# A two-layer decoder in one kernel: where the causal attention's projections, the head scalings and three of the layer norms stand in the program

## The reference, cut to what matters

```
# layer 0, first block: a linear recurrence over the 1024 tokens, then a small network
h = _ln(x, ln1_g, ln1_b); spec = einsum(h, W_to); real, imag = halves of spec
def step(carry, u):
    sr = sr * decay + r * 0.1;  si = si * decay + i * 0.1
    nr = clip(sr * c - si * s, -10, 10);  ni = clip(sr * s + si * c, -10, 10)
x2 = x + 0.1 * einsum(out_r|out_i, W_from)
h = _ln(x2, ln3_g, ln3_b); h = gelu(h @ W_ffn1.T + b1) @ W_ffn2.T + b2
return x2 + 0.1 * h                       # then x = _layernorm(x + this)
# layer 0, second block: cross attention, 16 heads of 16, over 154 context rows
# layer 1, first block: causal attention, 16 heads of 64 over 1024 tokens
att = where(causal, q k^T / 64, -inf); y = softmax(att) v; z = einsum(W, y) / 8
x = _layernorm(x + z)
```

## Time and profile before

| | us |
|---|---|
| median of three runs | 2289.43 |
| the profiled execution, its own time | 2288.46 |
| its span | 2286.7 |
| recurrence stage, while VectorE steps (61.8 to 623.5) | 561.7 |
| rest of the recurrence stage (to 711) | 87.5 |
| causal stage (904 to 1665) | 761 |

### The profile page before, as it was taken

The page is one execution under the profiler, slowest core; times in us unless marked ns, Lnnn a source line. Parts: engine busy times, 40 slices in busy tenths (PEclk is TensorE's granted clock), DMA queues, the critical chain, the costliest instruction groups (busy, mean ns, idle before and its releaser), DMA issues.

```text
span 2286.7 us, 34566 instructions
## 1 busy us (share of the span) xinstructions
PE 1815.0 (79%) x12969; PEld 1302.1 (57%) x12969; DVE 1445.2 (63%) x4633; ACT 934.0 (41%) x2211; POOL 501.3 (22%) x554
## 2 busy tenths in 40 slices
PE   4447666776677868998999789989887999998808
PEld 1335555655564435665666566666665899884306
DVE  4887787778723685565555345555654666663595
ACT  3413323332334742444444224444513555553662
POOL 3011110111010012333233223333321333330002
PEclk9667777877887987999999999999999999999958
DMA  4000000000000012000000000000032333310001
...
DMA packets 86312, 49.82 MB, mean 22 GB/s; under 512 B 40205, under 2 KB 83905, under 8 KB 85953
## 3 DMA queue, kind: packets, MB, share of 16 engines
...
q10 hardware_dynamic: 6784, 0.56, 0.3%
...
## 4 chain that ended last, share of the span: by engine, by line
PE 56%; DVE 23%; ACT 10%; issue 3%; POOL 2%; POOLq 0%; DVEq 0%; ACTq 0%
PE PS L1501 6%; PE PS L1795 5%; PE PS L1531 5%; PE PS L1518 4%; DVE sq L645 4%; DVE nx L642 4%; ACT px L1569 3%; PE PS L1468 3%; PE PS L1486 3%; PE PS L1476 3%; PE PS L2208 2%; PE PS L1546 2%; PE PS L1858 2%; PE PS L852 2%; PE PS L1814 2%
## 5 line engine op out<-in xcount | busy, mean ns | idle before, releaser
L1651 POOL TENSOR_SCALAR px<-px,crl 128x128 f32<-128x128 f32 (+7 forms) x128 | 239.8, 1874 | 461.1 <-DVE crl L1627 461.1
L1569 ACT ACTIVATE px<-PS,cnm 128x128 f32<-128x128 f32 (+7 forms) x256 | 187.6, 737 | 252.0 <-DVE cnm L1611 252.0
L1611 DVE TENSOR_REDUCE cnm<-PS 128x1 f32<-128x128 f32 (+7 forms) x256 | 181.9, 752 | 82.0 <-PE PS L1506 81.9
L182 POOL TENSOR_SCALAR rstd<-mv 128x1 f32<-128x1 f32 x128 | 41.3, 323 | 866.5 <-DVE mv L161 866.4
L645 DVE TENSOR_SCALAR sq<-nx 128x4 f32<-128x4 f32 x1024 | 183.1, 179 | 35.0
L642 DVE TENSOR_TENSOR_SCAN nx<-sq 128x6 f32<-128x6 f32 x1024 | 181.8, 178 | 34.7 <-SPq L2275 2.3
L1518 PE MATMUL PS<-ident,px 128*128 128x128 f32 x1152 | 160.5, 280 | 35.3 <-DVE pT L1619 33.5
L1518 PEld LDWEIGHTS PS<-ident,px 128*128 128x128 f32 x1152 | 130.7, 143 | 81.2 <-DVE pT L1619 37.3
L1501 PE MATMUL PS<-kT,qT 64*128 64x512 f32 (+3 forms) x768 | 159.5, 519 | 14.5 <-ACT px L1569 14.5
L1531 PE MATMUL PS<-pT,V 128*64 128x128 f32 x2304 | 159.1, 285 | 5.4 <-DVE pT L1619 5.3
L1885 ACT ACTIVATE YT<-YT,xnm 128x154 f32<-128x154 f32 x256 | 104.8, 414 | 92.9 <-DVE xnm L1927 92.9
...
## 6 DMA issues: line engine op xcount, KB each, us to landing
...
```

The source lines that it names most:

```text
L1569: e.activation(k.px[n % 2][:, h, 0:width], src, ACT.Exp, bias=k.cnm[:, n % 4, h:h + 1], accum_out=k.cl[:, n % 4, h:h + 1]).then_inc(sem("c ...
L1611: e.tensor_reduce(k.cnm[:, n % 4, h:h + 1], src, AX.X, ALU.max, negate=True).then_inc(sem("c.max"), 1)
L1651: e.tensor_scalar(k.px[n % 2][:, 0, 0:width], k.px[n % 2][:, 0, 0:width], k.crl[:, n % 4, 0:1], None, ALU.mult).then_inc(sem("c.normal0"), 1)
```

## The change

Three edits, and some semaphores that are shared.

1. **Norms 1, 2 and 3 change engine.** For these, VectorE's `unit` goes. GpSimd gets `shift`, which computes minus mean times reciprocal root (one 128x1 instruction), and ScalarE gets `side`, which applies scale and shift as one activation on 128x256.
2. **The recurrence's chains.** The norm's list reads r, stats, aggr, shift, 5 steps later side, 2 steps later turn and put. The end of "sums" (r 3 and its norm) becomes a fourth chain, "ends", offered 20 steps after `out`, and `out` comes 4 steps after `back`.
3. **The causal stage.** `cn` is parted by head: head 0's reciprocal stays ahead of `ct`'s copies, and head 1's reciprocal and scaling go behind them. The projections get fixed units: in units 2, 3, 4 of a pair its own second half, in 5, 6, 7 the next pair's first half. The 8 output tiles of batch 0 are spread, with `zout` and statistics in one unit, `unit` in the next and `turn` and `put` in the one after. The weight flips `wz` go to units 0 and 1 of pairs 1 and 2, and unit 0 of pair 3.

Semaphores `ident` and `rec.zero` go; what waited for them waits for `zeroed` and `zero`, the last of which is signalled after GpSimd's other opening memsets.

```
@@ norm_vector, norm_pool, norm_scalar @@
-        dst = k.xs4[:, lane, :] if L in (0, 1, 7) else k.xt(T)
+        dst = k.xs4[:, lane, :] if L in (0, 7) else k.xt(T)
+    def shift(L, T):
+        rs = k.rstd[:, lane_of(L, T), :]
+        w.wait_ge("ln.rstd", at("aggr", L, T))
+        e.tensor_scalar(rs[:, 0:1], k.mv[:, lane_of(L, T), 0:1], rs[:, 1:2], -1.0, ALU.mult, ALU.mult).then_inc(sem("ln.shift"), 1)
+    def side(L, T):
+        lane = lane_of(L, T)
+        w.wait_ge("ln.shift", at("shift", L, T))
+        if L == 1:
+            w.wait_ge("ln.turn", k.turn_before.get((L, T), 0))
+        dst = k.xs4[:, lane, :] if L == 1 else k.xt(T)
+        e.activation(dst, k.r4[:, lane, :], ACT.Identity, scale=k.rstd[:, lane, 1:2], bias=k.rstd[:, lane, 0:1]).then_inc(sem("ln.side"), 1)
@@ recurrence_order, network_chain, near_sums @@
+        needs["r", 3, T] = [("n.out", T)]
+    ends = Chain(o, needs, [step for T in k.near_tiles for step in near_ends(T)])
...
-        for kind, wait in (("r", gap), ("stats", 0), ("aggr", 0), ("unit", 5), ("turn", 0), ("put", 0)):
+        for kind, wait in (("r", gap), ("stats", 0), ("aggr", 0), ("shift", 0), ("side", 5), ("turn", 2), ("put", 0)):
...
-    yield 0, ("n.out", T)
-    yield 11, ("r", 3, T)
+    yield 4, ("n.out", T)
+
+
+def near_ends(T):
+    yield 20, ("r", 3, T)
     yield 1, ("stats", 3, T)
     yield 1, ("aggr", 3, T)
-    yield 5, ("unit", 3, T)
+    yield 0, ("shift", 3, T)
+    yield 6, ("side", 3, T)
@@ causal_order @@
-    def prepare(u):
-        return [[("cq", u, 0)], [("ck", u, 0)], [("cv", u, 0)], [("cq", u, 1)], [("ck", u, 1)], [("cv", u, 1)]]
...
+    for u in range(2 * HP):
+        for i, kind in enumerate(("cq", "ck", "cv")):
+            beside[u, 2 + i].append((kind, u, 1))
+            if u + 1 < 2 * HP:
+                beside[u, 5 + i].append((kind, u + 1, 0))
+    for x, steps in zip(((1, 0), (1, 1), (2, 0), (2, 1), (3, 0)), wz):
+        beside[x] += steps
+    for T in range(BT):
+        chain = list(norm_chain(5, T))
+        n = HP * BT + 2 + (0, 1, 1, 2, 3, 4, 5, 6)[T]
+        beside[units[n]] += [("zout", T), *chain[:3]]
+        beside[units[n + 1]].append(chain[3])
+        beside[units[n + 2]] += chain[4:]
+    o.add(("cq", 0, 0), ("ck", 0, 0), ("cv", 0, 0))
+    for n, x in enumerate(units):
+        o.add(("cs", *x))
         if n >= 2:
             o.add(("cp", *units[n - 2]))
-        for _ in range(min(total, 1 - (1 - total) * qt // (BT - 1)) - (total - len(rest))):
-            o.add(*rest.pop(0))
-        o.add(("cn", u, qt))
+        o.add(("cn", *x, 0), *beside[x])
         if n >= 1:
             o.add(("ct", *units[n - 1]))
+        o.add(("cn", *x, 1))
@@ causal_vector.cn @@
-        for h in range(2):
-            w.wait_ge("c.exp", 2 * n + h + 1)
-            e.reciprocal(k.crl[:, n % 4, h:h + 1], k.cl[:, n % 4, h:h + 1]).then_inc(sem("c.rl"), 1)
+        w.wait_ge("c.exp", 2 * n + h + 1)
+        e.reciprocal(k.crl[:, n % 4, h:h + 1], k.cl[:, n % 4, h:h + 1]).then_inc(sem("c.rl"), 1)
+        if h == 0:
+            return
```

65 lines of the change are left out of this document (29 added, 36 removed).

## The result

The changed kernel takes **2187.14 us** (median of 4 runs, 2185.94 to 2188.88) beside 2289.51 for the kernel before on the same chip: ratio 0.9554, 95% interval 0.9538 to 0.9571.

The account below looks back on a forecast made before the run. It took VectorE to bound the recurrence stage and TensorE the causal stage. Recurrence -11, causal waits -60 and clock -10 gave -81 on 2288.5, so 2207.5; with the median 1 us higher, 2208 us, range 2188 to 2246.

Parts of the forecast that it names:

- The recurrence term, -11: Recurrence stage: -13 us in the stepping part from `down` ending sooner after `r 1`, +2 behind the last step.
- its 13: Stepping part of the recurrence: 13 us shorter, about 2.2 in each of chunks 2 to 7, chunk 1 +0.3.
- A stepping part under 535 us: Sign that the recurrence forecast is wrong: the network (`down`) was not the next bound after `r 3`'s wait.
- my 548 to 552: Recurrence stage: the stepping part's length in us if the forecast is right.
- Causal waits, -60: Causal stage: TensorE's waits go, -37 in 12 usual pairs, -6 in pairs 0, 1 and 15, -17 in pair 8.
- The clock, -10: Causal stage: TensorE's granted clock, 0.98 on the mean, mostly comes back as waits go; -10 us, between 0 and -15.
- The light units 0 and 1: Rival, causal stage: units 0 and 1 of each pair, with less projection work, stall by 1.3 us each; 2250 us, chance 0.10.
- The slower case: Rival, causal stage: VectorE's head 1 scaling is blocked until GpSimd's scaling ends; 2336 us at 1.0 us a unit, chance 0.02.
- The recurrence gives its whole wait: Rival, recurrence stage: `down` moves up as far as VectorE does, -36 instead of -11; 2183 us, chance 0.09.
- The upper end of the range, 2246: Whole kernel: slow end of the 8-in-10 range, with half of the causal waits, no clock gain and recurrence -5.

Follow-up runs that it names:

- e14: e2 with 14 and 4 extra matmuls behind the score parts of batch 0's tiles, where TensorE stands for VectorE's maxima: 2198.13 us.
- e15: The kernel before, with `cp` of query tile 5 computed twice, about 1.5 us more TensorE work in unit 7 of the next pair: 2282.15 us.
- e1: The changed kernel with its causal edits undone, so only the recurrence edits (shift, side and chains) remain: 2266.99 us.
- e2: The changed kernel with its recurrence edits undone, so only the causal stage is changed: 2210.3 us.
- e3: The changed kernel with head 1's reciprocal and scaling again ahead of the copies of the transposed groups, projections in their new fixed units: 2219.08 us.
- e13: The changed kernel with batch 0's maxima asked for earlier, `mix` kept in place, `r 2` and batch 1's `normal` six steps later, and extra matmuls: 2156.09 us.

## Why the prediction was right in kind and short in size

**The recurrence term, -11, measured -19.9 with the opening and what follows the last step: the step that failed.** Its mechanism held in kind: `r 3` without a wait, `r 2` waiting 2.9 to 3.8 us for `down`, `r 1` 1.7 to 2.6 (foretold 2 to 3 each). The way round from one `r 1` to the next, in chunks 4 and 5, in us won (the last maxima are taken at the start of the last of the four instructions):

| | even: forecast | measured | odd: forecast | measured |
|---|---|---|---|---|
| `r 1` to `r 2` | 1.7 | 3.2 (34.6 to 31.4) | 2.5 | 1.1 (33.4 to 32.3) |
| `r 2` to the last maxima | 0.65 | 1.3 (25.6 to 24.3) | -0.1 | 0.4 (24.7 to 24.3) |
| last maxima to the next `r 1` | 0 | 1.1 (14.5 to 13.4) | 0 | -0.1 (14.0 to 14.1) |

(The terms of the forecast add up to 2.4 us a chunk, where I wrote about 2.2.) In the first row the two kinds of chunks together come out right, 4.3 against 4.2, but by luck. I gave the even chunks less, because I charged the moved `up` double at 1.2 GHz, and took TensorE's low clock as given: in the changed kernel `turned` is at full clock in every chunk, 2.2 instead of 4.0 us in the even ones, and in the odd ones a low stretch now covers `peak` (1.91 us instead of 1.60). e14 shows that this clock, and not the order, made the even chunks long. The third row I had called unchanged, from chunk 3 alone. Out of an even chunk TensorE was back at full clock 9.4 us after the last maxima started and is now after 7.1; out of an odd one after 8.5 and 8.7. So the error is again the clock, taken as fixed. The half microsecond or so too much in the second row, in both kinds of chunks, stays open. Together the rows give 2.2 us more for an even and an odd chunk than forecast, in three such pairs most of the 8.5 that the stepping part won beyond its 13. "A stepping part under 535 us" would have refuted the mechanism; it is 539.7, outside my 548 to 552 and on the mechanism's side.

**Causal waits, -60: right.** Usual pair 40.98 against 41 foretold. Pairs 0 to 14 listed 68.5 us of waits and list 3.2; TensorE's own work in a pair became 0.3 us longer, so some 61 us net. (Ahead of pair 0 5.1 us are saved, since three projections moved, and from pair 15 on 4.6 are lost.) Pair 8 has two waits of 0.5 us instead of eight with 18.1, and takes 66.8 us where I had foretold 78: some of its work moved on (pair 9 takes 45.6), and 7 us were clock.

**The clock, -10: the second term too small.** 15 us came back, the end of my range: 7.8 in pairs 1 to 6, as e15 shows by itself, and 7.3 in pairs 8 and 9 (28.3 us won, 21.0 of them waits). The row that I held against it, u=3 at clock 1.00 with all its waits, was a pair that escaped: with a wait of 2.3 us the clock fell in some pairs, not in all. The Trainium skill, "TensorE: Matmul & The Clock Gate", section "A second HAM failure mode: psum-queue depth-cycling", says that frequent micro-idles between groups of matmuls make the clock swing between its levels; the section that the prediction names tells it of longer waits, for DMA. The trace agrees in part: u=5 stands at 0.94 with a wait of 2.3 us and at 1.00 with 1.0, but u=3 and pairs 9 to 14 stand at 1.00 with 2.3.

**The ternary stage, -2.7, uncounted.** Its code is the same. TensorE, before and after:

```profile
719.70:891.90 172.20, 137.60 (x481) 73.37 (x481) 117.55 (x196) 91.40 (x139) 23.02 (x33) 0.83 0.09 19
```
```profile
699.80:869.30 169.50, 134.41 (x481) 72.17 (x481) 117.48 (x196) 91.52 (x139) 23.03 (x33) 0.84 0.09 19
```

The same 481 records take 3.2 us less at a slightly higher clock. It came with the recurrence edits (e1 has it, e2 not), but it does not need them: e14, whose recurrence differs from before by extra matmuls alone, has 169.3 too. Why the clock is higher there stays open.

**The rivals.** The light units 0 and 1 did not stall (no wait for px in the usual pair). The slower case did not come. In unit 7 head 1's scaling started only at GpSimd's end, but in e3 it stood inside GpSimd's scaling in all eight units, took its usual time (0.75 us at a width of 1024), and no pair was held up by it. The Trainium skill, "SBUF — State Buffer", section "SBUF: two separate sides", has the rule that, of certain VectorE instructions and a GpSimd one, the first to start fully blocks the other. One half of it shows, which the prediction had not looked for: where VectorE's scaling starts together with GpSimd's, GpSimd takes longer, and where it starts 0.2 to 1.0 us later (e3), it does not. A 128x896 scaling before, started with VectorE's (as 14 of 16 are), and in the changed kernel:

```profile
1117.37 3.00 POOL L1651 TENSOR_SCALAR px<-px,crl 128x896 f32<-128x896 f32 x1 [3.76 <-DVE crl L1627]
```
```profile
1111.66 2.52 POOL L1678 TENSOR_SCALAR px<-px,crl 128x896 f32<-128x896 f32 x1 [4.28 <-DVE crl L1650]
```

The other half, VectorE blocked until a GpSimd scaling that started first is done, shows in no row; two of VectorE's in pair 1 of the kernel before took 0.93 and 0.88 us instead of 0.62 and 0.69, and ended inside GpSimd's all the same. "The recurrence gives its whole wait" (2183) is nearest in time, but not in kind: waits of 33.5 us in all (5.2 before) stood in its place, and it took three more moves (e13) to be rid of them. (The upper end of the range, 2246, does not come out of its own terms: half of the causal waits, no clock and -5 give some 2249 to 2254.)
